# A fused language-model tower on one core: a batch's two value products move from the end of the batch before it to its own steps 1 and 2

## The reference, cut to what matters

```python
h = tok(x)            # emb[x] @ W_e2h, six layers x = (a * sigmoid(g) + x) * 0.7071 with
                      # (a, g) = conv1d(x, 3 taps, 128 -> 256), then @ W_h2e
xn = layernorm(h)
q1, k1, q2, k2, v = (heads(xn @ W) for W in (Wq1, Wk1, Wq2, Wk2, Wv))     # 8 heads of 16
attn1 = softmax(q1 @ k1.T * scale); attn2 = softmax(q2 @ k2.T * scale)
# window statistics of both (mean, std, max, min over 4 rows) -> small MLP -> alpha
fused = alpha * attn1 + (1 - alpha) * attn2
h = h + (fused @ v) @ Wo
h = h + ffn(layernorm(h))   # layernorm, attn_w, an expert's fc1 -> gelu -> fc2, next_w, gelu
```

## Time and profile before

| | |
|---|---|
| median of 3 runs | 5753.43 us (5746.42 to 5753.47) |
| profiled execution: time | 5751.02 us |
| its span | 5749.1 us |
| mean granted TensorE clock | 0.965 of full speed |
| ACT busy | 5228.8 us (91%) |
| PE busy | 5173.5 us (90%) |
| DVE busy | 5052.4 us (88%) |
| POOL busy | 2419.3 us (42%) |

### The profile page before, as it was taken

One profiled execution on the slowest core, in us unless ns is written; L12 is line 12 of the kernel. 1 busy time (PEld: TensorE's weight loads), 2 busy tenths in 40 slices (PEclk: granted clock), 3 DMA queues, 4 the chain that ended last, 5 costly groups with the idle time before them and its releaser, 6 DMA issues.

```text
span 5749.1 us, 118743 instructions
## 1 busy us (share of the span) xinstructions
PE 5173.5 (90%) x33798; PEld 2439.7 (42%) x33798; DVE 5052.4 (88%) x7409; ACT 5228.8 (91%) x7937; POOL 2419.3 (42%) x4456
## 2 busy tenths in 40 slices
PE   6999989989898998989889898998989899898996
PEld 4443434344353443435344353443434344343442
DVE  2989899998999999899998999999898998989982
ACT  2999999999999999999989999999999999999994
POOL 6525344252533525344352543525354352533523
PEclk8999999999999999999999999999999999999997
DMA  1111111111111111111111111111121111212110
GB/s 40 19 21 32 18 32 21 22 28 19 31 21 32 19 20 32 18 32 21 23 28 21 32 18 32 20 19 32 19 34 18 25 26 20 32 21 29 21 22 13
DMA packets 140246, 140.63 MB, mean 24 GB/s; under 512 B 64524, under 2 KB 83596, under 8 KB 139468
## 3 DMA queue, kind: packets, MB, share of 16 engines
q1 hardware_dynamic: 134428, 123.99, 15.5%
q0 software_dynamic: 4352, 8.92, 0.7%
q10 hardware_dynamic: 816, 0.02, 0.0%
HBM read 21.26 MB, written 8.91 MB: 5 GB/s over the span
## 4 chain that ended last, share of the span: by engine, by line
PE 42%; ACT 21%; issue 18%; DVE 11%; POOL 7%; ACTq 1%; DVEq 0%; POOLq 0%; DMA 0%; SPq 0%
PE ps_w L405 18%; PE ps_t L405 10%; ACT junk L599 9%; PE ps_o L405 8%; ACT exps L606 7%; PE ps_s L405 6%; DVE neg_s L744 5%; DVE rowmin L752 2%; ACT hpre L610 2%; DVE bn L764 1%; ACT chan L610 1%; ACT stage L610 1%; POOL part L890 1%; POOL odif L978 1%; POOL o L978 0%
## 5 line engine op out<-in xcount | busy, mean ns | idle before, releaser
L744 DVE TENSOR_SCALAR_CACHE_REDUCE neg_s<-ps_s 128x1024 f32<-128x1024 f32 x2048 | 2490.4, 1216 | 407.6 <-PE ps_s L405 329.9
L752 DVE TENSOR_REDUCE rowmin<-neg_s 128x1 f32<-128x1024 f32 x2049 | 2479.1, 1210 | 0.0
L599 ACT ACTIVATE junk<-neg_s,negmax 128x1024 bf16<-128x1024 f32 x2048 | 2354.6, 1150 | 78.9 <-DVE neg_s L744 72.7
L606 ACT ACTIVATE exps<-ps_t 128x1024 f32<-128x1024 f32 x2060 | 2112.2, 1025 | 145.7 <-PE ps_t L405 139.0
L405 PE MATMUL ps_o<-exps,v_cur 128*32 128x256 f32 x16512 | 1355.1, 401 | 199.3 <-DVE o_raw L760 164.6
L405 PE MATMUL ps_t<-qst,kst 99*128 99x512 bf16 x4120 | 1276.4, 392 | 212.0 <-ACT exps L606 208.9
L405 PE MATMUL ps_s<-kst,qst 96*128 96x512 bf16 x4096 | 1246.8, 386 | 18.3 <-DMA kst<-part 14.4
L405 PE MATMUL ps_w<-xc,cw 128*128 128x256 f32 x4704 | 1166.8, 384 | 4.4 <-DVE h L800 3.4
L405 PEld LDWEIGHTS ps_w<-xc,cw 128*128 128x128 f32 x4704 | 898.0, 192 | 225.9 <-DVE h L800 11.3
L405 PEld LDWEIGHTS ps_o<-exps,v_cur 128*32 128x32 f32 x16512 | 329.7, 109 | 1108.6 <-issue 629.7
L890 POOL TENSOR_SCALAR ctmp<-ug 128x256 f32<-128x256 f32 x408 | 164.6, 404 | 1470.1 <-ACT ug L681 1451.3
(11 more groups left out here) (183 smaller groups left out, 3871.2 us busy)
## 6 DMA issues: line engine op xcount, KB each, us to landing
qst<-part SPq DMA_DIRECT2D x257, 96.0 KB, 2.7
kst<-part SPq DMA_DIRECT2D x257, 96.0 KB, 2.9
qst<-part SPq DMA_DIRECT2D x257, 64.0 KB, 2.8
kst<-part SPq DMA_DIRECT2D x257, 64.0 KB, 2.8
qst<-mrow SPq DMA_DIRECT2D x1028, 1.5 KB
out_dram<-z SPq DMA_DIRECT2D x17, 512.0 KB, 3.2
qst<-part SPq DMA_DIRECT2D x257, 32.0 KB, 2.4
kst<-part SPq DMA_DIRECT2D x257, 32.0 KB, 2.5
```

Of the source, the lines that this page charges most:

```text
L599: nc.scalar.activation(junk[:, n % 2, :], neg_s[:, n % SLOTS_S, :], ACT.Exp, scale=-1.0, bias=negmax[:, r, t:t + 1], accum_out=sumsq[:, r, ...
L606: nc.scalar.activation(exps[:, n % RING, :], ps_t[:, :, :].rearrange("p c q -> p (c q)"), ACT.Exp, scale=0.5).then_inc(s_exp, 1)
L744: nc.vector.tensor_scalar(neg_s[:, n % SLOTS_S, :], ps_s[:, n % 2, :], -1.0, None, ALU.mult, ALU.min, accum_out=negmax[:, r, t:t + 1]).the ...
L752: nc.vector.tensor_reduce(rowmin[:, r, t:t + 1], neg_s[:, m % SLOTS_S, :], axis=AX, op=ALU.max, negate=True).then_inc(s_min, 1)
```

## The change

`v` 0 and 1 leave `PRE` and stand in the fixed table at steps 1 and 2 of the batch whose values they are; `vcopy` 0 moves from step 2 to 3, the four `QK[1]` products from 3, 5, 8, 10 to 4, 6, 9, 11. Two pauses of `GAP` are one step shorter. The waits are put to what now comes before.

```diff
-PRE = [("gather",)] + two("embT") + two("e2h") + CONV + two("h2e") + [("ln1",)] + two("xnT") + QK[0] + two("v")
+PRE = [("gather",)] + two("embT") + two("e2h") + CONV + two("h2e") + [("ln1",)] + two("xnT") + QK[0]
...
-       ("embT", 0): 1, ("e2h", 0): 2, ("conva", 0, 0): 2, ("h2e", 1): 3, ("ln1",): 2, ("xnT", 0): 5,
+       ("embT", 0): 1, ("e2h", 0): 2, ("conva", 0, 0): 2, ("h2e", 1): 2, ("ln1",): 1, ("xnT", 0): 5,
...
-    for n, task in {0: ("gather",), 2: ("vcopy", 0), 3: QK[1][0], 5: QK[1][1], 8: QK[1][2], 10: QK[1][3],
-                    14: ("vcopy", 1)}.items():
+    for n, task in {0: ("gather",), 1: ("v", 0), 2: ("v", 1), 3: ("vcopy", 0), 4: QK[1][0], 6: QK[1][1], 9: QK[1][2],
+                    11: QK[1][3], 14: ("vcopy", 1)}.items():
...
-BODY_TASKS = [("mrow", j) for j in range(U)] + [("unit", j) for j in range(U)] + QK[1] + POST + PRE
+BODY_TASKS = [("mrow", j) for j in range(U)] + [("unit", j) for j in range(U)] + two("v") + QK[1] + POST + PRE
...
                 elif kind == "v":            # PE
-                    w("act", ("xnT", tk[1]))
+                    w("act", None)
...
                 elif kind == "v":            # DVE
-                    if k == 0 and phase == "body":
-                        w("pool", ("vcopy", 1))
+                    if k == 0:
+                        w("pool", None)
...
                 elif kind == "vcopy":        # POOL
                     if tk[1] == 0:
-                        w("dve", None)
+                        w("dve", ("v", 1))
```

## The result

| | before | changed |
|---|---|---|
| median of 17 runs each | 5751.4 us (5744.32 to 5761.51) | 5762.44 us (5751.94 to 5766.71) |
| ratio | | 1.0017, 95% interval 1.0010 to 1.0024 |
| profiled execution: time, span | 5751.02, 5749.1 us | 5766.11, 5764.2 us |
| mean granted TensorE clock | 0.965 | 0.957 |
| busy: PE, ACT, DVE, POOL | 5173.5, 5228.8, 5052.4, 2419.3 us | 5191.9, 5227.6, 5055.7, 2419.8 us |

The change makes the kernel slower, by 0.17%: within the 0.2% that I had called "same" and inside the range, but on the other side of a forecast of 9.3 us gained. Its time is that of the rival called "the clock" (5761).

The account below looks back on a forecast made before the run. No engine bounds by share; DVE's 2.27 us step sets the basis, with waits for PE and sometimes POOL. Terms 8.9 + 5.9 + 4.8 + 2.7 - 13.0 gave 9.3 us gained: 5744 us, range 5729 to 5766.

Parts of the forecast that it names:

- the clock: Rival: TensorE's clock drop reaches the value products after the batch change in every batch, costing 17 us: 5761; chance 0.06.
- the copies and step 8: Copies leave steps 123 and 124 for 1 and 2, partly hidden in step 8's wait for msplit: 8.9 us gained.
- step 48: mrow 6 no longer waits 1.19 us for msplit; 0.75 left in four batches: 2.7 us gained.
- step 79: Its convolution goes, so ACT reaches the gelus of step 81 0.37 us sooner: 5.9 us gained.
- The view of what bounds the kernel: No engine by busy share; DVE ends each step, basis 2.27 us, waiting for PE's scores and, in few places, POOL.
- the loss of steps 90 to 107: Nine convolutions become eleven, none alone, pairs priced from steps 98 to 102: 13.0 us lost.
- Steps 13 to 15: Three convolutions become two, 8.06 us falling to 7.76 if ACT doesn't hold PE: 4.8 us gained.
- The gather: Rival: POOL's indirect DMA issues in steps 0 to 4 hold up the moved copies: 5769; chance 0.09 with other slower causes.
- Pairs covered: Rival: PE's lead carries over between convolution pairs in steps 90 to 107, so 13.0 us aren't lost: 5731; chance 0.28.

Follow-up runs that it names:

- replan_alone: Changed kernel with the value products back in steps 123 and 124 and their copy in step 2; 5760.23 us, 1.0018 of before.
- spread: Changed kernel with the eleven convolutions of steps 90 to 104 moved: two to 86 and 89, nine to the places of before; 5768.16 us, 1.0024 of before.
- warm_head: warm81_44 with one more constant matmul of 256 columns in each of steps 3 and 5; 5707.87 us, 0.9923 of the kernel before.
- v_alone: Kernel before with only the value products moved to steps 1 and 2, their copy to step 3; 5748.81 us, 0.9997 of before.
- before_warm: Kernel before plus six constant matmuls nobody reads, four in step 81, one each in 44 and 45; 5708.16 us, 0.9925 of before.
- warm81_44: Changed kernel plus six constant matmuls nobody reads, four in step 81, one each in 44 and 45; 5709.32 us, 0.9925 of before.

## Why the prediction was wrong, point by point

The forecast was 9.3 us gained, and the step lengths say 12.5 lost. Three terms carry the difference of 21.8, and the rest nearly cancels: the copies and step 8 (off by 7.6), step 48 (by 8.4), and step 79 (by 6.2). Each was read from one engine at one place, and booked as time that the kernel would get back.

**The view of what bounds the kernel, and the loss of steps 90 to 107: right.** 13.0 forecast, 13.8 measured, 14.0 in `replan_alone` and again with the clock held. The price of a pair read from steps 98 to 102 carried over: 94/95 cost 0.38 (0.30 forecast), 97/98 0.43 (0.59), 100/101 0.37 (0.30), 103/104 0.49 (0.50). `spread` shows the limit of the reading: the price is a matter of PE's lead at that place, and my guess that single convolutions are cheap anywhere was false.

**Steps 13 to 15: right**, -4.8 against -4.3.

**Step 79: the mechanism right, the end wrong.** "Its convolution goes ... 5.9 us" holds for ACT: with the clock held the stretch gains 6.4. (DVE's own step 79 fell from 2.92 to 2.28, by 0.64 where the bound assumed 0.57.) What failed is that I took the clock of step 81 as given. A step without a TensorE task ahead of a wait of 4 us is not only time given back. The clock fell earlier, `fc2` 0 ran more of its 5.8 us at 1.2 GHz, and 10.4 us were lost in step 81, of which 3 are the squares entering it later. The term is off by 6.2 us. The earlier trace rows has low windows of step 46 alone; a window of step 81 before, at 0.84, would have been the warning.

**The copies and step 8: the mechanism right, the gain eaten.** Eleven batches gain 7.4 us together, 0.16 to 0.20 in the typical ones (0.34 forecast: the stage copy came 0.15 later than I reckoned) and 0.7 to 1.4 in the late ones (1.15). The other five, 0, 5, 7, 12 and 14, lose 7.2; the end of the last batch gives 1.2. In three of them the clock stands at 0.59 in step 6, after step 5, which has no TensorE task any more, and POOL's split waits for the stage copy; the counts under `warm_head` support that cause. In the other two the value product of step 1 meets a low clock: step 1 takes 3.90 us in batch 0 (clock 0.65) and 3.07 in batch 12 (0.84), where 2.84 is usual. That wasn't tried by itself. And `v_alone` shows that the term had a hole: what a wait on DVE is worth can't be read from DVE alone when ACT uses the same pause.

**Step 48: the wait went, the time stayed.** Its mean fell from 2.97 to 2.76, 3.3 us (2.7 forecast). The step of the prediction that failed is "so 0.75 is left": it took DVE's wait in step 48 for time lost, and PE uses it to run ahead of the convolutions of steps 50 to 54. In the three batches of before in which step 48 waits in full (3.69), steps 49 to 57 take 22.70, in the others mostly 23.63; in the changed kernel 23.69. PE's lead shows it directly: its scores for step 49 end 0.97 us ahead of the start of that step in batch 5 of before, and 0.04 in the changed kernel. So the 3.3 came back as 3.8 there. The kernels with the clock held show it over all batches: `before_warm` has a mean of 3.71 in step 48 and 22.7 in 49 to 57, `warm81_44` 2.76 and 23.7, and steps 45 to 57 have the same length, 33.92 and 33.96. The rest of the miss is steps 46 and 47, 5.2 longer, with step 46 at a low clock in more batches (3.41 to 3.65). With the clock held that is gone; why the clock fell there more often in this trace stays open, since no step from 18 to 46 lost a task.

**The rivals.** "The clock" had 0.06 and the time, 5761 against 5762.4, for a reason that isn't its own: it placed the loss on the value products in steps 1 to 3 of every batch, and steps 1 and 2 are 2.84 and 2.87 long in the undisturbed batches. The match of the time is luck. The granted clock did fall somewhere in steps 125 to 3 at more changes of batch (12 of 15, 4 before), but it lengthened the value product of step 1 in batches 0, 8 and 12 alone, 2.0 us together. The right rival would have been the same mechanism at the steps that lose their TensorE task ahead of a wait: 79 and 5. "The gather" (0.09) is refuted by the 0.68 us of the copies. "Pairs covered" (0.28) is refuted by the 13.8.

## What to carry to other kernels

When a plan moves TensorE's tasks, list the steps that lose one, and see in the windows what the granted clock does in the step after each and whether TensorE ends last there; price both levels. Where TensorE has to wait some microseconds for another engine in each iteration and its work afterwards is on the path, a few matmuls on constants during the wait can pay: six a batch, in three steps, gave 0.8% here, more than the change under study could win or lose. Before a wait is booked as slack to be filled, look for which other engine catches up or gets ahead in it: ACT in step 8, PE in step 48.

## What was not expected of the hardware

Constant matmuls in three steps raised the granted clock of those steps from 0.50 to 0.84 up to 1.00, and brought three kernels 42 to 45 us under the kernel before. The Trainium skill ("TensorE: Matmul & The Clock Gate", section "HAM oscillation — how this bites in real kernels") describes a TensorE that waits between groups of matmuls and begins each group at the low clock, and advises to reorder the loop or enlarge the work; the trace agrees with the effect (5.83 us for eight records, 3.96 with the clock up), and here neither remedy was needed.

The clock also goes with the time of one and the same kernel: over the 17 runs of the changed kernel the fastest, 5751.94 us, has a mean granted clock of 0.961, and the slowest, 5766.71 us, one of 0.956. And a raised clock was worth nothing where TensorE doesn't end last: in steps 123 to 127 it went from 0.86 to 1.00 at 12.23 and 12.22 us.
